# VectorE's product with C of a split column as two half products, in a fused Mamba and RWKV layer

## The reference

```
xz = x_in @ W_in;  x, z = halves of xz
proj = x @ W_x;    B_ssm, C_ssm = its last 2 * 16 columns
delta = softplus(proj[:, :256] @ W_dt + b_dt)
for each time step and each state n:
    h[d, n] = exp(delta[d] * A[d, n]) * h[d, n] + delta[d] * x[d] * B_ssm[n]
    y[d]   += h[d, n] * C_ssm[n]
y = (y + x * D_param) * silu(z) @ W_out; then layer norm, gain and bias
# then: token mixing with the previous token, r = sigmoid(.), k = relu(.)^2, out = r * (k @ W_v.T)
```

## Time and profile before

| what | value |
| --- | --- |
| median of 3 runs | 968.0 us (966.49 to 968.97) |
| the profiled execution | 967.01 us |
| its span, first to last instruction | 965.1 us |
| DVE busy | 904.4 us (94%), 922 instructions |
| PE, POOL, ACT busy | 893.8, 892.3, 852.8 us |
| granted TensorE clock, mean | 0.979 |

### The profile page before, as it was taken

How to read it: one execution, slowest core, us unless ns; L and a number is a source line. 1 busy time by engine, 2 the same in 40 slices (tenths; PEclk the granted TensorE clock), 3 DMA queues, 4 the chain that set the end, 5 groups by cost and what they waited for, 6 DMA issues and landing times.

```text
span 965.1 us, 15450 instructions
## 1 busy us (share of the span) xinstructions
PE 893.8 (93%) x4834; PEld 697.5 (72%) x4834; DVE 904.4 (94%) x922; ACT 852.8 (88%) x2060; POOL 892.3 (92%) x401
## 2 busy tenths in 40 slices
PE   8676878999999999999999999999999999999997
PEld 4355575868878686887868677786867778688886
DVE  4899999999999999999999999999999999999765
ACT  4586989999999999998999999998999999978855
POOL 3899999999999989999999989999999999999960
PEclk9896998999999999999999999999999999999999
DMA  6344455462645644364464626446443744553320
GB/s 209 156 168 176 172 209 199 165 222 97 246 152 195 242 176 174 134 246 171 175 242 179 222 86 245 155 193 241 180 170 147 255 165 163 218 189 139 131 77 23
DMA packets 49793, 171.44 MB, mean 178 GB/s; under 512 B 4721, under 2 KB 30577, under 8 KB 33457
## 3 DMA queue, kind: packets, MB, share of 16 engines
q1 hardware_dynamic: 48384, 169.13, 47.6%
q0 software_dynamic: 512, 1.31, 0.4%
q10 hardware_dynamic: 816, 0.02, 0.1%
HBM read 153.15 MB, written 9.44 MB: 168 GB/s over the span
## 4 chain that ended last, share of the span: by engine, by line
PE 32%; DVE 30%; ACT 27%; issue 9%; DMA 1%; DVEq 0%; SPq 0%; ACTq 0%
DVE da_ps L1031 13%; ACT da_ps L654 9%; PE w_ps L1295 9%; DVE hg L1031 8%; DVE hg L1038 7%; PE w_ps L1302 6%; PE y_ps L1286 5%; ACT xn_tok L593 3%; PE w_ps L1311 3%; PE w_ps L1314 3%; ACT h_tok L607 2%; PE w_ps L1320 2%; ACT xres L860 1%; PE w_ps L1376 1%; PE da_ps L1295 1%
## 5 line engine op out<-in xcount | busy, mean ns | idle before, releaser
L541 POOL TENSOR_TENSOR dbx<-u,b_ring 128x1024 f32<-128x1024 f32 x255 | 599.2, 2375 | 14.9 <-DVE hg L1031 7.6
L654 ACT ACTIVATE da_ps<-delta,a_neg 128x512 f32<-128x512 f32 x512 | 338.1, 682 | 21.4 <-DVE hg L1038 8.5
L554 POOL TENSOR_TENSOR hg<-hg,c_ring 128x1024 f32<-128x1024 f32 x123 | 292.0, 2374 | 9.3 <-ACT carry L660 8.1
L1286 PEld LDWEIGHTS y_ps<-ident,hg 128*128 128x128 f32 x2048 | 237.8, 144 | 44.0 <-issue 29.9
L1286 PE MATMUL y_ps<-ident,hg 128*128 128x128 f32 x2048 | 259.0, 277 | 11.4 <-POOL hg L554 8.4
L1031 DVE TENSOR_TENSOR_SCAN da_ps<-da_ps,carry,dbx 128x512 f32<-128x512 f32 x200 | 246.9, 1274 | 3.8 <-ACT da_ps L654 3.2
L1031 DVE TENSOR_TENSOR_SCAN hg<-da_ps,carry,dbx 128x512 f32<-128x512 f32 x184 | 224.3, 1265 | 1.8 <-ACT da_ps L654 1.6
L1038 DVE TENSOR_TENSOR hg<-da_ps,c_ring 128x1024 f32<-128x1024 f32 x132 | 161.0, 1220 | 8.8 <-DVE da_ps L1031 0.5
L1031 DVE TENSOR_TENSOR_SCAN da_ps<-da_ps,dbx 128x512 f32<-128x512 f32 x64 | 75.8, 1215 | 4.2 <-ACT da_ps L654 4.1
L1031 DVE TENSOR_TENSOR_SCAN hg<-da_ps,dbx 128x512 f32<-128x512 f32 x64 | 75.4, 1211 | 0.6 <-ACT da_ps L654 0.3
L1295 PE MATMUL w_ps<-xnT,w_in 128*128 128x512 f32 x120 | 59.3, 618 | 8.2 <-ACT xT L696 8.2
(11 more groups left out here) (206 smaller groups left out, 1340.5 us busy)
## 6 DMA issues: line engine op xcount, KB each, us to landing
c_ring<-bc_rows_dram SPq DMA_DIRECT2D x64, 1024.0 KB, 4.8
b_ring<-bc_rows_dram SPq DMA_DIRECT2D x63, 1024.0 KB, 6.6
xres<-in_L_attn_x_in_dram SPq DMA_DIRECT2D x16, 512.0 KB, 4.7
x_tok<-in_L_attn_x_in_dram SPq DMA_DIRECT2D x15, 512.0 KB, 6.4
res<-xn_tok SPq DMA_DIRECT2D x15, 512.0 KB, 3.2
out_dram<-r_out SPq DMA_DIRECT2D x15, 512.0 KB, 3.2
bc_rows_dram<-bc_rows SPq DMA_DIRECT2D x16, 64.0 KB, 6.5
w_in<-in_L_attn_W_in_dram SPq DMA_DIRECT2D x2, 256.0 KB, 5.3
```

The source lines that it names most:

```text
L541: pool.tensor_tensor(dbx[:, n % X_RING, :, :], u[:, ip, :, :], b.to_broadcast([P, KH, LC]), ALU.mult).then_inc(s["dbx_done"], 1)
L554: pool.tensor_tensor(part, part, c_of(n).to_broadcast([P, KH, LC]), ALU.mult).then_inc(s["g_pool"], 1)
L654: act.activation(da_of(n, h), delta[:, ip, h, :], ACT.Exp, scale=a_neg[:, h, n:n + 1]).then_inc(s["da_ready"], 1)
L1286: last = pe.matmul(y_tok[:, b, h * P:(h + 1) * P], hg[:, n % H_RING, h, b * P:(b + 1) * P], ident[:, :], is_transpose=True, start=n == 0 a ...
```

## The change

In a split column where no other operation stands between the scans and the product (no entry of the table at place 2n), the product is made as two operations of 512 elements, one per half. Each waits for the scan of its own half. The semaphore `g_vec` is raised once, by the second. These are columns 0, 2, 5, 12 and 14 of every chunk before the last, and all five split columns of the last.

```diff
+            def times_c_by_halves(t, n):
+
+                need(dve, c_loaded[n // GN], 16 * (t + 1))
+                for h in range(KH):
+                    need(dve, s["scan_done"], KH * (NS * t + n) + h + 1)
+                    at = (KH * n + h) % DA_BANKS
+                    last = dve.tensor_tensor(hg[:, n % H_RING, h:h + 1, :], da_ps[:, at:at + 1, :], c_of(n), ALU.mult)
+                last.then_inc(s["g_vec"], 1)
+
...
                     if scan and after and n in split_of(t):
-                        times_c(t, n)
+                        if 2 * n in of_step(t, VEC_HEAD, VEC_TURN, VEC_TAIL).values():
+                            times_c(t, n)
+                        else:
+                            times_c_by_halves(t, n)
```

## The result

The changed kernel took 962.1 us (median of 6 runs, 960.15 to 962.83), the kernel before, run beside it, 968.1 us (6 runs, 966.49 to 968.97). The ratio is 0.994, with a 95% interval from 0.9927 to 0.9952. A second series of runs gave 961.3 against 967.8 us, 0.9933 (0.9919 to 0.9947). The change made the kernel faster by 6 us, 5.9 and 6.5 in the two series; 4.5 were forecast.

A forecast was written before the change was run, and what follows sets the result against it. DVE was fullest (904.4 of 965.1 us), PE and ACT close behind; PE sets the last chunk's end. Of 12.8 us saved, 1.0 (start-up) + 3.5 (steady) = 4.5 arrives: 967.0 to 962.5, plus 1.0 to the median, 963.5; range 959.5 to 967.6.

The forecast's parts named there:

- The column: On DVE, two scans and their product in a halved column take 3.55 us, 3.71 before: 0.16 saved.
- (a): Column 2 of each odd chunk, where ACT waits 1.20 us for DVE right after: 0.32 us kept per four chunks.
- (b): Chunk 5, columns 12 and 14, and chunk 6's column 0: 0.20 us kept together, 0.05 of it after column 12.
- (c): Chunk 6 columns 12 and 14 and chunk 7 column 0: between 0 and 0.48 us kept, taken as 0.15.
- (d): Chunk 7, ACT's waits behind columns 12 and later and for chunk 8's column 0, plus column 5: 0.50 us kept.
- DVE's waits for ACT: Some 8 us more in total than before, at columns 6, 12 and 15 of even chunks.
- (e): Chunks 0 and 1, where ACT waits for six halved products by 0.54 us or more: 1.0 us kept.
- PE's stream as closed: From chunk 14 on PE runs without a wait, so nine later halved products of chunks 14 and 15 are worth nothing.
- All of it arriving: The whole 12.8 us saved on DVE reaches the end: 955.2 us; chance 0.15, shared with 6 to 12 us arriving.
- a slower kernel: Halves on DVE get no cover from the scan, +0.10 us a column: 970.8 us; chance 0.06.
- Rival 2: DVE's saving turns into waits for ACT's exponentials, only start-up keeps something: 967.0 us, up to 968; chance 0.24.
- the columns called lost: Even chunks' columns 2, 5, 12, 14 and the next column 0: saving runs into PE's and ACT's streams, some kept in (b)-(d).

The follow-up runs named there:

- late_halves: The change, but both halves wait for the second scan: 969.35 us against 967.79 for the kernel before, ratio 1.0022.
- all_halves: The change, with all 132 products halved, also the 52 that stand behind another operation: 961.98 us.
- the repeated pair: The changed kernel and the kernel before run once more with no edit: 961.28 us (5 runs) and 966.38 us (one run).
- no_even_2_5: The change, with columns 2 and 5 of even chunks made whole products again: 961.55 us.
- the pair with one table: The kernel before and the changed kernel, each with ACT's softplus made a ReLU and its first table load removed: 967.52 and 959.8 us.
- before_one_table: The kernel before, with ACT's softplus made a ReLU and its first table load removed: 967.52 us.

## Why the prediction was right, and where it was off

**The column.** 3.71 to 3.55 us was right to 0.02 in the rows, and late_halves shows its cause: the same count of operations without the early start costs 0.06 more than the whole product. The next operation starts 1.18 us after a half pair whose rows last 1.27, and in the products' rows it is the wait for the engine's own last scan that brings the pause of 0.10 and takes the overlap away. The Trainium skill (VectorE: DVE Perf Modes, "The DRAIN you can't avoid") has the next operation start only when the pipe is empty. The same section adds what the prediction left out, "A next op that is not held starts earlier", and with that the trace agrees (0.59 us from start to start for halves that last 0.68). The rule in "Rules for kernel authors" of that page of the Trainium skill, to minimise the count of operations and not of semaphores, speaks against the change, and here the measurement decides against it. Where another operation already covers the last scan, the runs agree with it: all_halves took 0.45 us more per four chunks.

**What arrives in the steady part.** Forecast 1.17 us per four chunks, measured 1.24 (1.34 by the repeated pair). Step by step, DVE's first scans of five columns, chunk 8 column 7, chunk 9 column 7, chunk 10 column 7, chunk 11 column 3 and chunk 12 column 7, before:

```profile
504.14 1.21 DVE L1031 TENSOR_TENSOR_SCAN hg<-da_ps,dbx 128x512 f32<-128x512 f32 x1
...
560.87 1.27 DVE L1031 TENSOR_TENSOR_SCAN hg<-da_ps,carry,dbx 128x512 f32<-128x512 f32 x1
...
616.62 1.27 DVE L1031 TENSOR_TENSOR_SCAN hg<-da_ps,carry,dbx 128x512 f32<-128x512 f32 x1
...
657.77 1.28 DVE L1031 TENSOR_TENSOR_SCAN da_ps<-da_ps,carry,dbx 128x512 f32<-128x512 f32 x1
...
728.72 1.21 DVE L1031 TENSOR_TENSOR_SCAN hg<-da_ps,dbx 128x512 f32<-128x512 f32 x1
```

and after:

```profile
501.93 1.21 DVE L1031 TENSOR_TENSOR_SCAN hg<-da_ps,dbx 128x512 f32<-128x512 f32 x1
...
558.55 1.27 DVE L1031 TENSOR_TENSOR_SCAN hg<-da_ps,carry,dbx 128x512 f32<-128x512 f32 x1
...
613.93 1.27 DVE L1031 TENSOR_TENSOR_SCAN hg<-da_ps,carry,dbx 128x512 f32<-128x512 f32 x1
...
654.83 1.28 DVE L1031 TENSOR_TENSOR_SCAN da_ps<-da_ps,carry,dbx 128x512 f32<-128x512 f32 x1
...
725.25 1.21 DVE L1031 TENSOR_TENSOR_SCAN hg<-da_ps,dbx 128x512 f32<-128x512 f32 x1
```

The lead is 2.21, 2.32, 2.69, 2.94 and 3.47 us, so it grows by 0.11, 0.37, 0.25 and 0.53.

| stretch | forecast | measured |
| --- | --- | --- |
| (a) column 2 of chunk 9 | 0.16 | 0.11 |
| (b) column 12 of chunk 9 to column 0 of chunk 10 | 0.20 | 0.37 |
| (c) and (a): columns 12, 14 of chunk 10, 0 and 2 of chunk 11 | 0.31 | 0.25 |
| (d) the rest of chunk 11, column 0 of chunk 12 | 0.50 | 0.53 |

(a) shows in ACT's own row, which stood at 1.20 us in the earlier trace rows:

```profile
323.82 0.17 ACT L665 ACTIVATE carry<-da_ps 128x2 f32<-128x2 f32 x1 [1.03 <-DVE hg L1038]
```

0.17 less, one product's saving. Of (b), ACT's wait of 0.15 at 355.63 is gone in the changed kernel, and (b) is the one term of the steady part that was mis-sized: I took 0.05 of the possible 0.32 for column 14 and the next column 0, and about 0.2 came. That even chunks lose columns 2 and 5 was right (no_even_2_5), and the streams of ACT and PE that the prediction named meet at column 6, where the softplus waits for PE's chain and the exponentials stand behind it (the pair with one table). Which part of the two streams would have to shrink for these columns to count is not shown: no run had less work on PE in front of column 6, or went without the second load. DVE's waits for ACT grew by 6.7 us where I forecast 8. In DVE's scans they grew mostly at columns 6 (2.2 us) and 15 (1.5), as forecast, hardly at 12 (0.2), and, not forecast, at columns 1 and 3 (1.4 and 0.7) and by 1.0 at `mixed`. PE's wait for `xn_tok` stayed (1.75 us at 317.25, against 1.67 in the earlier trace rows).

**The odd pause.** From chunk 4 to chunk 8 the kernel before took 224.91 us, 0.35 us more than from 8 to 12; the changed one takes 223.32 both times. The 0.35 are one pause. DVE before, chunk 6, column 14:

```profile
416.39 1.27 DVE L1031 TENSOR_TENSOR_SCAN da_ps<-da_ps,carry,dbx 128x512 f32<-128x512 f32 x1
418.11 1.23 DVE L1038 TENSOR_TENSOR hg<-da_ps,c_ring 128x1024 f32<-128x1024 f32 x1 [0.46 <-DVE da_ps L1031]
```

After, the first half starts 1.18 us after this scan (415.14 and 416.32), with no pause. The 0.46 us had been put aside in the forecast as one odd wait. 0.35 of them, what they have beyond the usual 0.10, are part of the gain.

**Start-up and end.** (e), 1.0 us for chunks 0 and 1, is the term that came out least well in the traces. In the profiled pair the lead was 0.78 us at column 3 of chunk 2 (first scans at 151.33 and 150.55 us) and gone, -0.50, one column later (154.38 and 154.88). DVE's row there, in the changed kernel:

```profile
154.19 0.75 DVE L1084 SCALAR_TENSOR_TENSOR mixed<-w_ps,muk,mixed 128x512 f32<-128x512 f32 x1 [1.13 <-ACT mixed L710]
```

ACT in turn waits 1.23 us for PE (152.98), whose transposes of `xn_tok` last 1.94 us (148.38) against 1.06 in the kernel before (149.00). The stretch from 140 to 150 us of the changed kernel, with the columns of the earlier trace rows; the kernel before has a granted clock of 0.83 there:

```profile
140.00:150.00 10.00, 5.13 (x28) 4.55 (x26) 9.57 (x11) 9.59 (x22) 10.00 (x5) 0.66 0.25 87
```

This one wait is also the 1.0 us at `mixed`. The repeated pair has the same wait, at 0.66 against 0.81; its lead goes from 0.26 to -0.92 us. Whether the change brings the low clock about is not shown: over all traces with halves it lay between 0.60 and 0.91 in this stretch, over those with whole products between 0.76 and 1.00. So the lead at the start of chunk 4 was 0.48 us (254.38 and 253.90) in the first pair and 0.0 in the repeated one, where the forecast had 1.6 (1.0 and half of 1.17). By the medians the change is worth 1.5 to 2.4 us more than by the profiled pairs (4.35, and 966.38 less 962.23, 4.15). Whether that is the true share of start-up in other executions, or the spread of single executions, whose first four chunks differ by 1 us and more between runs of one kernel, stays open. At the end 0.40 us came after column 7 of chunk 14, where I had counted PE's stream as closed and nothing as kept.

**The sum.** The profiled pair had 4.35 us where 4.5 were forecast, and the terms behind that are 1.1 less up to chunk 4, 0.5 more from chunk 4 to 12 (0.35 the odd pause, the rest the steady part) and 0.4 more from there to the end. The mechanism and the steady part were right; that the total came out close owes something to misses that cancel. The medians lie 1.4 us below the forecast time, and no trace shows where that difference lies.

**The rivals.** All of it arriving (955.2) and a slower kernel (970.8) didn't come; the latter asked for halves more than 0.75 us apart, and they are 0.59 apart in every one of the 80 columns. Rival 2, a saving turned into waits for ACT, is what happens to the columns called lost, 6.7 us in all, but the waits that I had counted on did give theirs.

## What to carry to other kernels

On an engine with one long queue, look for an operation that waits for the engine's own last result: here each such wait cost 0.20 us, a pause of 0.10 and the lost overlap. Cutting the consumer so that its first part needs only the older result can be worth it where no other operation already stands between the two (here 0.16 us a column), and costs 0.06 us per cut where one does. With the engines at 93% side by side a third to a half of the saving arrived here (4.3 us in the trace, 6 by the medians, of 12.8). The places are found by the waits on both sides: those that fall on the engine that is served, and those that rise on the engine that was made faster. Their sums over the whole kernel are a rough guide only.

## What the runs showed of the hardware

- An operation of 1,024 elements from PSUM takes 1.14 us from start to start, two of 512 take 1.18 to 1.21. Halves whose first waits for the scan before the last start 0.59 us apart, halves that both wait for the last scan 0.61.
- The pause before the product of column 14 in chunk 6, 0.46 us in place of 0.10, stood at the same place in all five traces with whole products (from 416.56 to 418.95 us), in late_halves in chunk 9 instead, and in none whose first half starts early. The row names DVE's own scan as what it waited for. Its cause was not found, and no run was made on it.
- The steady part repeats to 0.14 us, while the first scan of a kernel began at 27.1 to 27.5 us in twelve traces and at 29.05 and 31.76 us in two (before_one_table, no_even_2_5): a difference of 2 to 3 us between two single runs says nothing here, distances inside the trace do.
